# Cross-attention and a mixture of experts on one core: experts chosen in groups of four tiles, and another order of work in the late attention

## The chip, the cores and the metric

One core of a Trainium2 chip runs the whole kernel in one launch. The metric is the time of an execution on the device in microseconds (us). The kernel before was run three times: 351.25, 352.0 and 418.66 us, median 352.0. The profiled execution is the one of 351.25 us; its span from the first to the last instruction is 349.4 us.

Engines as in the profile: PE is TensorE (matmuls), PEld its weight loads, DVE is VectorE, ACT is ScalarE, POOL is GpSimd, SP is the engine that issues most DMAs.

## The reference

x is 32 tiles of 128 tokens with 256 channels, in float32. Per token the reference computes a layer normalisation, and an attention over the token's own 16 heads of 16 channels: Q from the normalised token, K and V from the context token at the same place, a 16 by 16 matrix of logits, softmax, values, the output projection Wd, and the residual. Then, on a second layer normalisation, it chooses one of 8 experts per token (argmax of 8 gate logits), runs that expert's two-layer network (256 to 512 to 256, exact GELU), scales by the softmax score and adds the residual.

```python
query = q @ Wq.T + bq; key_p = k @ Wk.T + bk; value = v @ Wv.T + bv     # heads: (.., 16, 16)
logits = einsum('bsid,bsjd->bsij', query, key_p) / sqrt(16)
out = einsum('bsij,bsjd->bsid', softmax(logits), value) @ Wd.T + bd
x = x + out
idx, scores = argmax(gates), max(gates)            # gates = softmax(layernorm(x) @ w_red @ wg_n.T)
o = gelu(h @ W1[idx] + b1[idx]) @ W2[idx] + b2[idx]
x = x + o * scores
```

## The kernel before

Attention runs in iterations t = 0 to 41 (`*_attention` on each engine), software-pipelined: every engine has its own written order of work, and semaphores tie them together. Iteration t treats several tiles at once. Tile t is projected to K, V and Q (`tensor_project`, L1088, L1091, L1185), evicted by VectorE (`vector_kv` L599, `vector_q` L605, L610), stored to a scratch in HBM by SP and loaded back in another layout. Tile z = t-5 has its K expanded by GpSimd with a mask (`pool_expand`, L413) and its V copied by ScalarE (`scalar_pad`, L973). Tile s0 = t-6 gets its logits (L1100), the row maximum (L631) and subtraction (L633) on VectorE, the exponential on ScalarE (L927), and the sum, reciprocal and product on VectorE (`normed`, L566, L569, L573). Tile s1 = t-7 is transposed (`tensor_turn`, L1197), expanded with a mask in four blocks (`expand` on VectorE, L558, `scalar_expand` on ScalarE, L996, one instruction a block), multiplied with V (L1111) and copied out by ScalarE (L950). Tile w = t-8 gets the output projection (L1143), the residual (L644), the largest gate logit (L649) and, on GpSimd, the gate logits less the largest (L452). Tile d = t-9 gets its norm from a power on GpSimd (L430, L432, L435) that waits for ScalarE's moments (L902) of the iteration before, and ScalarE's score row (`scalar_row`). Its row goes to HBM by SP (`sync_row`). GpSimd also adds the bias to tile t-2's residual (L449) and reorders a context tile (`pool_context`, L398).

Who expands which block is told by `blocks`: in the steady iterations ScalarE has 3 and VectorE 1, from iteration 27 (ROUTE) ScalarE has all 4, in 34 and 35 (FIRST = 34) each has 2, then VectorE all. VectorE comes first, ScalarE waits for it. Outside iterations 32 and 33 ScalarE's blocks follow its exponential.

Experts are worked on in slots of 128 rows. The first 13 slots (S1) are filled from the first 20 tiles (R1), so that their routing can run during the attention: `vector_early` with parts 0 to 7. Part 0 (iteration 28) chooses the expert of all 20 tiles (L692, L693, L694); TensorE counts (`tensor_counts_a`); part 1 (end of 28) turns the counts into prefixes and full tiles (L698 to L705); parts 2, 3, 4 (iterations 29, 30, 31) work out every token's place (L707 to L722) and the list of experts (L723 to L726); parts 5 and 6 (32, 33) build selection matrices (L730 to L736), TensorE inverts the list with 20 small matmuls (`tensor_inverse_a`, L1223) and part 7 (34) turns the result into addresses (L744, L745). GpSimd's first gather (`pool_ffn(0)`, L497) of iteration 34 needs these. `after` makes each step wait for the one before. `PIECES` makes GpSimd's K expansion of iterations 28 to 34 wait for VectorE's part of that iteration.

`FILLS` are filler transposes of the identity (L1059) that nobody reads, {7: 16, 32: 6, 33: 6, 35: 6} before the values matmul. From iteration 36 the expert slots run: rows transposed (L1290), first layer (L1278), GELU (L1051), second layer (L1328), bias and score (L889, L895), scatter (L472); weights are copied by L859 or L1032.

## Time and profile before

| what | value |
|---|---|
| median of the runs | 352.0 us |
| time of the profiled execution | 351.25 us |
| its span | 349.4 us |
| PE busy | 326.0 us, 93% of the span |
| DVE busy | 250.7 us, 72% |
| ACT busy | 200.4 us, 57% |
| POOL busy | 270.2 us, 77% |
| chain that ended last | PE 69%, DVE 9%, DMA 8%, issue 5%, ACT 4%, POOL 3% |
| moved by DMA | 63.46 MB, mean 182 GB/s |

The shares are means over stages that have different limits. The chain that ended last is followed back from the last instruction: at each step to what released it, or to the instruction before it on its engine. "issue" is time in which the engine waited for nothing that the profile shows. The timeline gives each instruction, or a few alike, with its start and duration; the stretch table gives busy time, granted TensorE clock (1.00 is full speed, 2.4 GHz) and the DMA engines' busy share between two times.

### The profile page before, as it was taken

Reading aid. Unit: us, or ns where it says so; the run is one execution under the profiler, and the core shown is the slowest. Engines: PE = TensorE matmul, PEld = TensorE weight load, DVE = VectorE, ACT = ScalarE, POOL = GpSimd, SP = SyncE. Lnnn points to the kernel's source line nnn. Section 1 sums busy time; section 2 is a strip of 40 time slices with the busy share of each in tenths; the row PEclk is TensorE's granted clock in tenths of the full one; section 3 lists DMA queues with packets and bytes.
Section 4 is the critical chain, followed back from the end, with each engine's and each line's share of the span. In section 5 each row is a group of like instructions: output and inputs, shape, how many; then the busy total and the mean of one; then the engine's idle time right before and its main releaser. Section 6 shows DMA issues by size and latency. Waiting matters only on the chain.

```text
span 349.4 us, 11007 instructions
## 1 busy us (share of the span) xinstructions
PE 326.0 (93%) x3731; PEld 273.2 (78%) x3731; DVE 250.7 (72%) x717; ACT 200.4 (57%) x533; POOL 270.2 (77%) x523
## 2 busy tenths in 40 slices
PE   6999899999999999899687899979999999999993
PEld 5787788888888888677476688968898999995682
DVE  6656788888888888899777656875765566554652
ACT  1001678777877787578754745784567535435431
POOL 3598789999999899787888767774778777777634
PEclk9999999999999999999969999999999999999998
DMA  6699898999999999999997111251122222222200
GB/s 223 233 294 301 264 217 249 268 301 271 264 270 262 291 328 322 340 237 251 303 364 289 50 33 46 68 153 48 46 76 66 77 65 73 77 61 74 62 15 31
DMA packets 54839, 63.46 MB, mean 182 GB/s; under 512 B 36334, under 2 KB 45695, under 8 KB 54784
## 3 DMA queue, kind: packets, MB, share of 16 engines
q1 hardware_dynamic: 50544, 52.77, 51.8%
q0 software_dynamic: 3456, 9.12, 8.8%
q10 hardware_dynamic: 784, 0.87, 0.7%
q8 instruction: 31, 0.51, 0.6%
q14 instruction: 24, 0.20, 0.2%
HBM read 41.59 MB, written 21.68 MB: 181 GB/s over the span
## 4 chain that ended last, share of the span: by engine, by line
PE 69%; DVE 9%; DMA 8%; issue 5%; ACT 4%; POOL 3%; ACTq 1%; SPq 1%; DVEq 0%; POOLq 0%
PE bQ L1328 14%; PE bY L1143 7%; PE bKV L1091 7%; PE bKV L1088 7%; PE bQ L1185 7%; PE bKV L1278 6%; PE bL L1278 6%; PE bO L1111 4%; PE bL L1100 4%; PE bA L1197 3%; DMA r<-row_scr,ig 3%; PE bT L1290 2%; DMA xt<-in_x 2%; DMA r<-in_xc 2%; DMA b2b<-in_bd_col 1%
## 5 line engine op out<-in xcount | busy, mean ns | idle before, releaser
L1328 PE MATMUL bQ<-w,wA 128*128 x264 | 63.2, 382 | 2.1 <-issue 1.2
L413 POOL TENSOR_TENSOR x<-ql,mask 128x1024 f32<-128x1024 f32 x32 | 60.6, 1893 | 4.7 <-DVE texp L726 1.7
L1328 PEld LDWEIGHTS bQ<-w,wA 128*128 128x128 f32 x264 | 47.5, 190 | 9.5 <-issue 4.3
L472 POOL DMA_INDIRECT out<-r,isc x36 | 38.7, 1074 | 19.6 <-issue 17.6
L973 ACT ACTIVATE pad<-ql 64x512 f32<-64x512 f32 x64 | 40.0, 626 | 22.3 <-DMA ql<-qkv_scr 21.9
L889 DVE TENSOR_TENSOR r<-bQ,b2b 128x256 f32<-128x256 f32 (+1 forms) x39 | 16.6, 425 | 36.2 <-PE bQ L1328 34.3
L497 POOL DMA_INDIRECT r<-row_scr,ig x36 | 37.4, 1038 | 5.7 <-issue 2.4
L996 ACT ACTIVATE ax<-bA,mask 128x256 f32<-128x256 f32 x92 | 36.7, 474 | 0.7 <-DVE ax L558 0.5
L1143 PE MATMUL bY<-wD,oT 128*128 128x265 f32 x128 | 35.7, 402 | 1.0 <-ACT oT L950 0.8
L1278 PEld LDWEIGHTS bL<-wA,r 128*128 128x128 f32 x272 | 32.7, 192 | 2.4 <-issue 1.7
L1278 PE MATMUL bL<-wA,r 128*128 128x128 f32 x272 | 33.4, 276 | 1.1 <-ACT r L1032 1.1
L1185 PE MATMUL bQ<-wA,r 128*128 128x265 f32 x128 | 33.9, 387 | 0.3 <-DVE wA L533 0.3
L1088 PE MATMUL bKV<-wA,r 128*128 128x256 f32 x128 | 33.0, 380 | 1.1 <-DMA r<-in_xc 0.7
L1091 PE MATMUL bKV<-wA,cp 128*128 128x256 f32 x128 | 33.1, 381 | 0.0
L927 ACT ACTIVATE bX<-bL 128x256 f32<-128x256 f32 x32 | 11.8, 370 | 36.9 <-DVE bL L633 36.9
L432 POOL TENSOR_TENSOR cat<-ve,half 128x2 f32<-128x2 f32 x42 | 30.2, 720 | 3.5
L1051 ACT ACTIVATE wA<-bL,r 128x128 f32<-128x128 f32 x68 | 19.4, 373 | 22.1 <-PE bL L1278 22.1
L1278 PEld LDWEIGHTS bKV<-wA,r 128*128 128x128 f32 x256 | 30.8, 192 | 1.2 <-issue 0.4
L1278 PE MATMUL bKV<-wA,r 128*128 128x128 f32 x256 | 31.5, 276 | 0.0
L1051 ACT ACTIVATE wA<-bKV,r 128x128 f32<-128x128 f32 x64 | 18.2, 366 | 21.1 <-PE bKV L1278 21.0
L1007 ACT ACTIVATE r<-r 128x256 f32<-128x256 f32 x36 | 22.0, 611 | 11.2 <-DMA r<-row_scr,ig 10.9
L1185 PEld LDWEIGHTS bQ<-wA,r 128*128 128x128 f32 x128 | 24.1, 189 | 4.3 <-DVE wA L533 0.4
(214 smaller groups left out, 703.6 us busy)
## 6 DMA issues: line engine op xcount, KB each, us to landing
qkv_scr<-qkv SPq DMA_DIRECT2D x16, 768.0 KB, 4.4
ql<-qkv_scr SPq DMA_DIRECT2D x32, 384.0 KB, 5.8
r<-in_xc SPq DMA_DIRECT2D x15, 512.0 KB, 6.0
row_scr<-cat SPq DMA_DIRECT2D x32, 133.5 KB
w1b<-in_W1b SPq DMA_DIRECT2D x8, 514.0 KB, 7.3
w<-in_W SPq DMA_DIRECT2D x8, 512.0 KB
xt<-in_x SPq DMA_DIRECT2D x15, 256.0 KB, 6.0
b2b<-in_b SPq DMA_DIRECT2D x2, 512.0 KB, 8.2
```

The source lines that it names most:

```text
L413: eng.tensor_tensor(quarter(kx[:, z % 2, :]), spread(ql[z // 2 % 2][:, :, z % 2, 0:HD]), mask_k, ALU.mult).then_inc(S["kx"], 1)
L472: eng.indirect_dma_start(out, bass.IndirectOffsetOnAxis(ap=isc[k][:, :], axis=0), yo[k], None, bounds_check=NTOK - 1, oob_is_err=False).th ...
L497: eng.indirect_dma_start(gr[k], None, row_scr[0:R1 * P] if a < S1 else row_scr, bass.IndirectOffsetOnAxis(ap=ig[k][:, :], axis=0)).then_in ...
L973: i_ = eng.activation(pad[n, z % 3, :].rearrange("p (k g h d) -> p k g h d", k=2, g=NG_, h=2) [:, :, :, h, :], ql[z // 2 % 2][n, :, z % 2, ...
L996: i_ = eng.activation(quarter(ax[:, :])[:, :, b, :], bA[:, 0:C].rearrange("p (g i) -> p g i", g=NG_), ACT.Copy, scale=mask4[:, b:b + 1])
L1051: i_ = eng.activation(hT[a % 2][:, k, :], bH[a % 2][:, k * P:(k + 1) * P], ACT.Gelu, bias=w1s[a % 2][:, KC * HID + k:KC * HID + k + 1])
L1088: eng.matmul(bKV[:, 0:C], xcT[:, a % XC, KC + k, :], wT[:, k, 0:C], start=(k == 0), stop=(k == KC - 1))
L1091: i_ = eng.matmul(bKV[:, C:2 * C], cp[a % 2][:, k, :], wT[:, k, C:2 * C], start=(k == 0), stop=(k == KC - 1))
L1143: i_ = eng.matmul(bY[:, 0:EXT], oT[:, k, :], wD[:, k, :], start=(k == 0), stop=(k == KC - 1))
L1185: i_ = eng.matmul(bQ[:, 0:EXT], xcT[:, a % XC, k, :], wT[:, k, 2 * C:3 * C + NL], start=(k == 0), stop=(k == KC - 1))
L1278: i_ = eng.matmul(bH[a % 2][:, k * P:(k + 1) * P], w1s[a % 2][:, c * HID + k * P:c * HID + (k + 1) * P], gT[a % 2][:, c, :], start=(c == 0 ...
L1328: i_ = eng.matmul(bQ[:, 0:C], hT[b % 2][:, k, :], w2[:, bass.ds(eb * (KH * C) + k * C, C)], start=(k == 0), stop=(k == KH - 1))
```

## The change

The choice of experts is cut into five groups of four tiles: `vector_choice(g)` runs in iterations 13, 17, 21, 25 and 28 (`GROUP_AT`), after the residual of that iteration. Part 1 of the early routing copies the prefixes out of PSUM before it scans, and rounds the counts to whole tiles by adding and subtracting a large constant, in place of a comparison and a sum. TensorE's output projection of iteration 29 waits for the scan. The list of experts (end of part 4) and the number taken (end of part 6) become part 8, in iteration 34 after the softmax; part 7, the addresses, moves ahead of the residual of iteration 34.

In `scalar_attention`, the blocks of iteration 7 and of 32 to 35 come ahead of the exponential, V's copies of iterations 32 on come behind it, and the output copy of 32 to 35 comes ahead of the moments. In 34 and 35 VectorE's blocks wait for ScalarE's. Iteration 7's four blocks are all ScalarE's. GpSimd's K expansion of iterations 32 and 33 comes behind the power; its waits on pieces of the routing end with iteration 31. The filler transposes become {7: 10, 32: 4, 33: 4, 35: 4}.

```diff
...
 STEADY = FIRST + 2
-FILLS = {7: 16, 32: 6, 33: 6, 35: 6}
+FILLS = {7: 10, 32: 4, 33: 4, 35: 4}
 FILLS_ROWS = 8
...
 BLOCKS_STEADY, BLOCKS_ROUTING, BLOCKS_DRAIN = 3, 4, 2
+TURNED_FIRST = (7, *range(NT, STEADY))
+OUTPUT_FIRST = range(NT, STEADY)
 SELR = NH2 + 2
-PIECES = (("gsub", R1), ("rv_a", 5), ("rv_a", 10), ("rv_a", 13), ("texp_a", 1), ("selk_a", 1), ("taken_a", 1))
+GROUP = 4
+GROUPS = R1 // GROUP
+GROUP_AT = {min(GROUP * g + 13, ROUTE + 1): g for g in range(GROUPS)}
+SCANNED = 2 * GROUPS + 1
+RV_COUNTS = SCANNED + 2
+PIECES = (("gsub", R1), ("rv_a", RV_COUNTS), ("rv_a", RV_COUNTS + 5), ("rv_a", RV_COUNTS + 8))
 
...
                 n, v, w, d, z = t + 1, t - 2, t - 8, t - 9, t - 5
-                if live(z) and t >= NT:
+                if t >= FIRST and live(z):
                     pool_expand(eng, t, z)
...
                     pool_constants(eng)
-                if live(z) and t < NT:
+                if live(z) and t < FIRST:
                     pool_expand(eng, t, z)
...
                 return 0
-            return BLOCKS_DRAIN if s1 + 7 >= FIRST else BLOCKS_ROUTING if s1 + 7 >= ROUTE else BLOCKS_STEADY
+            return BLOCKS_DRAIN if s1 + 7 >= FIRST else BLOCKS_ROUTING if s1 + 7 >= ROUTE or s1 == 0 else BLOCKS_STEADY
 
...
                 eng.wait_ge(S["tr_a"], s1 + 1)
+                if 0 < b and s1 + 7 in TURNED_FIRST:
+                    eng.wait_ge(S["axs"], by_scalar(s1))
                 if s1 > 0:
...
                     expand(eng, s1)
+                if t == ROUTE + 7:
+                    vector_early(eng, 7)
                 if live(s0) and t <= ROUTE:
...
                     normed(eng, s0)
-                if t == ROUTE + 1:
-                    vector_early(eng, 0)
+                if t in GROUP_AT:
+                    vector_choice(eng, GROUP_AT[t])
                 if live(a) and t >= 7:
...
                         vector_stats(eng, a + 2)
-                if ROUTE + 1 < t <= ROUTE + 7:
+                if ROUTE + 1 < t < ROUTE + 7:
                     vector_early(eng, t - ROUTE)
+                if t == ROUTE + 7:
+                    vector_early(eng, 8)
                 if live(a) and t >= 7:
...
 
-        def vector_early(eng, part):
+        def routed(eng):
             def after(i_):
...
                 eng.wait_ge(S["rv_a"], rv_a[0])
-
-            if part == 0:
+            return after
+
+        def vector_choice(eng, g):
+            after = routed(eng)
+            n = slice(GROUP * g, GROUP * (g + 1))
+            if g == 0:
                 eng.wait_ge(S["const"], 1)
                 eng.wait_ge(S["wide"], 2)
-                eng.wait_ge(S["gsub"], R1)
-                after(eng.scalar_tensor_tensor(key_a, glog[:, 0:R1, :], 0.0, io_e[:, 0:R1, :], ALU.is_ge, ALU.mult))
-                after(eng.tensor_reduce(top_a, key_a, AX, ALU.max))
-                eng.tensor_tensor(oh[:, 0:R1, :], key_a, top_a.unsqueeze(2).broadcast_to((P, R1, NE)),
-                                  ALU.is_equal).then_inc(S["oh_a"], 1)
+            eng.wait_ge(S["gsub"], GROUP * (g + 1))
+            after(eng.scalar_tensor_tensor(key_a[:, n, :], glog[:, n, :], 0.0, io_e[:, n, :], ALU.is_ge, ALU.mult))
+            after(eng.tensor_reduce(top_a[:, n], key_a[:, n, :], AX, ALU.max))
+            eng.tensor_tensor(oh[:, n, :], key_a[:, n, :], top_a[:, n].unsqueeze(2).broadcast_to((P, GROUP, NE)),
+                              ALU.is_equal).then_inc(S["oh_a"], 1)
+
+        def vector_early(eng, part):
+            after = routed(eng)
             if part == 1:
                 eng.wait_ge(S["cnt_a"], 1)
+                eng.tensor_copy(pre_a, bA[:, C:C + NE * R1].rearrange("p (e n) -> p e n", e=NE)
+                                ).then_inc(S["cnt_r"], 1)
                 after(eng.tensor_tensor_scan(inc_a.rearrange("p e n -> p (e n)"),
...
                                              bY[:, EXT:EXT + NE * R1], 0.0, ALU.mult, ALU.add))
-                eng.tensor_copy(pre_a, bA[:, C:C + NE * R1].rearrange("p (e n) -> p e n", e=NE)
-                                ).then_inc(S["cnt_r"], 1)
-                after(eng.scalar_tensor_tensor(gtm_a, inc_a[:, :, R1 - 1:R1].broadcast_to((P, NE, R1)), 1.0 - P,
-                                               io_m[:, :, 0:R1], ALU.add, ALU.is_gt))
-                after(eng.tensor_reduce(full, gtm_a, AX, ALU.add))
+                after(eng.tensor_scalar(fexc, inc_a[:, :, R1 - 1], (1.0 - P) / 2, ROUND, ALU.add, ALU.add))
+                after(eng.tensor_scalar(full, fexc, ROUND, None, ALU.subtract))
             if part == 2:
...
                 after(eng.tensor_tensor(fexc, finc, full, ALU.subtract))
-                after(eng.tensor_scalar(pinc, finc, float(P), float(S1 * P), ALU.mult, ALU.min))
-                after(eng.scalar_tensor_tensor(exc_a, fexc.unsqueeze(2).broadcast_to((P, NE, R1)), float(P), inc_a,
-                                               ALU.mult, ALU.add))
+                after(eng.tensor_scalar(pinc, finc, float(S1 * P), None, ALU.min))
+                after(eng.tensor_tensor(exc_a, fexc.unsqueeze(2).broadcast_to((P, NE, R1)), inc_a, ALU.add))
                 eng.wait_ge(S["cnt_r"], 1)
...
                 after(eng.tensor_tensor(posr_a, pos_a, posk_a, ALU.subtract))
+            if part == 8:
                 after(eng.tensor_tensor(tcmp_a, pinc.unsqueeze(1).broadcast_to((P, S1, NE)),
...
                 eng.tensor_scalar(texp[:, 0:S1], tsum_a, float(NE - 1), None, ALU.min).then_inc(S["texp_a"], 1)
+                after(eng.tensor_scalar(pexc, fexc, float(S1 * P), None, ALU.min))
+                eng.tensor_tensor(taken[:, :], pinc, pexc, ALU.subtract).then_inc(S["taken_a"], 1)
             if part in (5, 6):
...
                                   ALU.mult).then_inc(S["selk_a"], 1)
-            if part == 6:
-                after(eng.tensor_scalar(pexc, fexc, float(P), float(S1 * P), ALU.mult, ALU.min))
-                eng.tensor_tensor(taken[:, :], pinc, pexc, ALU.subtract).then_inc(S["taken_a"], 1)
             if part == 7:
...
                 a, z, s0, s1, w, d = t, t - 5, t - 6, t - 7, t - 8, t - 9
-                if live(z) and t >= NT:
-                    scalar_pad(eng, z)
-                if live(s1) and shared(s1) and NT <= t < FIRST:
+                if live(s1) and t in TURNED_FIRST:
                     scalar_expand(eng, s1)
...
                                    ACT.Exp, scale=HD ** -0.5).then_inc(S["exp"], 1)
-                if live(s1) and shared(s1) and not NT <= t < FIRST:
+                if live(s1) and shared(s1) and t not in TURNED_FIRST:
                     scalar_expand(eng, s1)
-                if live(z) and t < NT:
+                if live(z):
                     scalar_pad(eng, z)
...
                         scalar_weights(eng, s)
+                if live(s1) and t in OUTPUT_FIRST:
+                    scalar_output(eng, s1)
                 if live(w):
...
                     scalar_row(eng, t, d)
-                if live(s1):
-                    eng.wait_ge(S["pvo"], s1 + 1)
-                    if s1 > 0:
-                        eng.wait_ge(S["wd"], s1)
-                    eng.activation(oT[:, :, :].rearrange("p m (i b) -> p m i b", i=NH),
-                                   bO[:, 0:C].rearrange("p (m b i) -> p m i b", m=KC, i=NH),
-                                   ACT.Copy).then_inc(S["oT"], 1)
+                if live(s1) and t not in OUTPUT_FIRST:
+                    scalar_output(eng, s1)
                 for s in SLOTS_AT.get(t, ()):
...
                 eng.wait_ge(S["score"], d + 1)
+
+        def scalar_output(eng, s1):
+            eng.wait_ge(S["pvo"], s1 + 1)
+            if s1 > 0:
+                eng.wait_ge(S["wd"], s1)
+            eng.activation(oT[:, :, :].rearrange("p m (i b) -> p m i b", i=NH),
+                           bO[:, 0:C].rearrange("p (m b i) -> p m i b", m=KC, i=NH),
+                           ACT.Copy).then_inc(S["oT"], 1)
 
...
             eng.wait_ge(S["tr_a"], s1 + 1)
-            if blocks(s1) < NC_:
+            if blocks(s1) < NC_ and s1 + 7 not in TURNED_FIRST:
                 eng.wait_ge(S["axv"], by_vector(s1))
...
                     eng.wait_ge(S["oT"], w + 1)
+                    if t == ROUTE + 2:
+                        eng.wait_ge(S["rv_a"], SCANNED)
                     for k in range(KC):
...
         def tensor_counts_a(eng):
-            eng.wait_ge(S["oh_a"], 1)
+            eng.wait_ge(S["oh_a"], GROUPS)
             eng.wait_ge(S["const"], 1)
...
             eng.matmul(bY[:, EXT:EXT + NE * R1], ones[:, :], ohe_a, start=True, stop=True).then_inc(S["cnt_a"], 1)
```

## Rows read from the trace of the kernel before

**Rows 1.** Stretches: length, busy PE PEld DVE ACT POOL, clock, DMA share, GB/s

```profile
100.00:141.00 41.00, 41.00 (x724) 33.92 (x724) 36.16 (x108) 32.32 (x85) 37.13 (x68) 1.00 1.04 296
...
170.00:190.00 20.00, 16.08 (x295) 13.11 (x294) 14.72 (x41) 11.60 (x31) 17.96 (x27) 0.83 1.05 355
...
177.30:182.60 5.30, 5.26 (x76) 4.53 (x76) 3.17 (x10) 3.41 (x9) 4.72 (x7) 0.50 1.00 361
```

**Rows 2.** The chain of waits, whole span: start us, us, what

```profile
57.11 0.91 PE bY L1143 x4
...
140.98 1.04 PE bY L1143 x4
...
148.18 0.90 PE bY L1143 x4
...
153.44 1.13 PE bY L1143 x4
...
164.54 1.89 POOL x L413
...
169.75 1.57 ACT ax L996 x4
...
179.15 1.25 POOL r L497
...
185.42 5.83 DMA r<-row_scr,ig
```

**Rows 3.** The timeline of a steady iteration: start us, us, engine, line, operation

```profile
51.87 0.42 DVE L631 TENSOR_REDUCE mx<-bL 128x16 f32<-128x256 f32 x1
...
52.83 1.89 POOL L413 TENSOR_TENSOR x<-ql,mask 128x1024 f32<-128x1024 f32 x1
...
54.90 0.69 DVE L599 TENSOR_TENSOR qkv<-bKV,bqkv 128x512 f32<-128x512 f32 x1
...
55.15 0.75 POOL L449 TENSOR_TENSOR xt<-xt,bdb 128x265 f32<-128x265 f32 x1
...
56.11 0.63 PE L1100 MATMUL bL<-x,pad 128*32 128x64 f32 x32
...
56.81 0.42 DVE L631 TENSOR_REDUCE mx<-bL 128x16 f32<-128x256 f32 x1
```

**Rows 4.** The timeline of iterations 28 and 29

```profile
143.74 0.45 DVE L692 SCALAR_TENSOR_TENSOR r<-glog,io_e 128x160 f32<-128x160 f32 x1
...
144.31 0.74 POOL L449 TENSOR_TENSOR xt<-xt,bdb 128x265 f32<-128x265 f32 x1
...
144.59 0.65 DVE L694 TENSOR_TENSOR oh<-r 128x160 bf16<-128x160 f32 x1
...
148.31 0.42 DVE L631 TENSOR_REDUCE mx<-bL 128x16 f32<-128x256 f32 x1
```

**Rows 5.** Groups of VectorE instructions by line: count, busy us, mean ns

```profile
L761 DVE TENSOR_TENSOR oh<-pad 128x96 bf16<-128x96 f32 x1 | 0.2, 250 | 0.0
...
L709 DVE TENSOR_SCALAR r<-r 128x8 f32<-128x8 f32 x1 | 0.2, 172 | 0.0
...
L703 DVE SCALAR_TENSOR_TENSOR r<-r,io_m 128x160 f32<-128x160 f32 x1 | 0.3, 317 | 0.0
```

**Rows 6.** The timeline of iterations 31 to 34

```profile
163.59 0.27 DVE L723 TENSOR_TENSOR r<-r,io_k 128x104 f32<-128x104 f32 x1
...
166.70 0.72 POOL L432 TENSOR_TENSOR cat<-ve,half 128x2 f32<-128x2 f32 x1
...
171.42 0.65 PE L1111 MATMUL bO<-ax,pad 128*32 128x64 f32 x32 [0.92 <-issue]
...
175.09 1.35 PE L1223 MATMUL bKV<-r 128*128 128x26 bf16 x20
...
178.11 0.17 DVE L745 SCALAR_TENSOR_TENSOR idg<-bKV,r 128x13 int32<-128x13 f32 x1
```

**Rows 7.** The timeline of iteration 8's beginning, TensorE

```profile
41.30 0.65 PE L1100 MATMUL bL<-x,pad 128*32 128x64 f32 x32 [0.45 <-issue]
```

## The prediction

> **What bounds the kernel now.** I read the stretch table first [rows 1]. Between 100 and 141 us TensorE is busy for all 41.00 us at full clock: the steady attention iterations are bound by its matmuls. The other engines are not idle either: VectorE is busy 36.16 of 41.00, GpSimd 37.13, and the DMA engines are full. Then the chain of waits [rows 2]: the output projection L1143 starts at 57.11 in iteration 11 and at 140.98 in iteration 28, so 17 iterations take 83.87 us, 4.93 each. The next two take 7.20 (to 148.18) and 5.26 (to 153.44). From 141 to about 192 the chain leaves TensorE: it goes over GpSimd's K expansion at 164.54, ScalarE's four blocks at 169.75, GpSimd's first gather at 179.15 and the landing of the second, issued at 185.42 and 5.83 us under way. After that it is TensorE's expert matmuls again. So this change, which touches iterations 7, 13 to 28 and 28 to 35, can win between 141 and 192 us and can lose in the steady part.
>
> How much room the steady part has is read from one iteration [rows 3]. The row maximum L631 starts at 51.87, and the projection of the next iteration must start at 57.11 [rows 2]: 5.24 us. What that path needs is seen in iteration 29, where VectorE sets the pace: L631 at 148.31 [rows 4], the projection at 153.44 [rows 2], 5.13 us with four blocks on ScalarE. Four blocks take 1.57 [rows 2], 0.39 each; with three the path is 4.74, and some 0.1 more for the wait on VectorE's own block. So L631 may come about 0.4 late before TensorE waits. VectorE itself is idle 4.84 us in 8.3 iterations [rows 1], 0.58 each, mostly the short gaps between dependent instructions; I estimate 0.2 as true spare ahead of L631 at 56.81 [rows 3].
>
> **Part by part. Choices in groups, steady part.** In iterations 13, 17, 21 and 25 VectorE gets three dependent instructions of 32 elements between L649 and L599 at 54.90. Of 96 elements one costs 0.25, of 8 elements 0.17 [rows 5]: 0.19 each, 0.6 together, if nothing is in the way. Something is: GpSimd's residual bias L449 runs from 55.15 to 55.90 [rows 3], where the third would run. In iteration 28 the same instruction, L694, ran beside L449 and took 0.65 [rows 4]; 96 elements without company took 0.25 [rows 5], so 160 should take 0.32. It ended at 145.24, 0.19 after L449. Put at 55.35, it would end near 56.09 in place of 55.55: 1.1 us are inserted. So L631 is late by 0.4 (0.6 less the spare 0.2) up to 0.9, and TensorE loses 0 to 0.5 per group. I take 0.3, nearer the hindered end since that is the row I have: four groups, **+1.2** (0 to +2.0). Who else stands behind it on VectorE: K/V eviction L599, the statistics for GpSimd's power, the Q eviction and with it SP's store of the record (all four iterations are odd). Each of these has its reader an iteration or more away, so I cost them at nothing; GpSimd's K expansion, which would come 1 us late, ends 1.4 ahead of its logits today (52.83 + 1.89 against 56.11 [rows 3]). The groups are four iterations apart, enough to lose the lag again.
>
> The Trainium skill ("SBUF — State Buffer", section "SBUF: two separate sides") says that VectorE and GpSimd share one pair of ports by an exclusive lock, which a VectorE instruction with two SBUF inputs needs and for which the loser fully blocks. L694 and L449 agree with it. By that rule alone each group would cost its full 0.5, and the sum below would be 0.8 higher.
>
> **Iteration 28.** Before, L692 at 143.74 to the end of L694 at 145.24 is 1.50 [rows 4]; a group of four takes 0.6 to 1.3 there, again beside L449. I take 0.3 saved (0.15 to 0.9). The count of full tiles replaces L703 (0.32) and a reduction as long by two instructions of 8 elements at 0.17 [rows 5]: 0.3. The copy out of PSUM goes ahead of the scan, so the transposes no longer wait for the scan; the projection now waits for it instead, and behind that wait stand TensorE's K/V and Q matmuls. The scan is over as early as before, so this costs nothing by itself; if it came late it would cost its own half microsecond. L631 of iteration 29 comes 0.6 early.
>
> **Iteration 31.** Three instructions of the expert list, from L723 at 163.59 [rows 6], 0.7 together, leave the space ahead of the Q eviction. They return in iteration 34, after the softmax. With the 0.6 the next L631 is 1.3 early. Parts 2 and 3 keep their number of instructions.
>
> **Iterations 32 and 33.** Today GpSimd waits for that list before K (164.54 [rows 2]), the power L432 follows at 166.70 [rows 6], the moments wait for it and the output copy for the moments; ScalarE fills V ahead of its blocks, which start at 169.75 [rows 2], and the values matmul of iteration 33 is at 171.42 [rows 6]. With the new order the blocks start when the transposes are done, near 168.0, and the values matmul near 169.65: 1.8 early. K comes later in GpSimd's order, by power and its product, 1.3 us. It starts near 164.6, as now, and TensorE gets logits only 0.5 early. V's copies, two of 0.63 per tile, lie after the exponential and end about when K does. SP's load of the last record waits for its store's landing, not for these. The output copy goes ahead of the moments, which feed the next power; with the power early they still end before GpSimd gets there. In 34 and 35 VectorE's two blocks wait for ScalarE's two instead of the other way round: the same two pieces in the other order, 0.
>
> The waits of K on the pieces fall away from iteration 32 on, so K may now hold up the selection matrices. Nothing in the trace has them side by side; from below it costs nothing, from above the rest of a K expansion, 1.9. Two GpSimd instructions (K's tail and L449) can meet it: I take 0.5.
>
> **Iteration 34.** The inverse matmul goes from 175.09 [rows 6] to about 173.7. The addresses L745, at 178.11 now, stand behind the residual, its maximum and the softmax, 1.7 us; ahead of them they come 1.4 after the matmuls start and are done near 175.5, 2.7 early. For that VectorE stands 0.8 idle with the residual queued behind, which still starts earlier than now. GpSimd can use 2.7 only if it is free: K, power and product end near 176.0 to 176.8. The first gather is issued near 177.2 instead of 179.15 [rows 2], the second 1.9 before its 185.42 [rows 2], and what follows hangs on the second one's landing. **−1.9** for 141 to 192 us, all of the parts above together (−1.2 to −2.7).
>
> **Iteration 7 and the filler transposes.** The first tile's four blocks go ahead of the exponential. I estimate the values 0.5 early, but the softmax 0.9 late, and VectorE's lateness reaches V's copies two tiles on. The wait of 0.45 before the logits at 41.30 [rows 7] shrinks. 0 (−0.3 to +0.2). The 12 filler transposes that go run while TensorE would wait anyway: 0, as long as the clock stays up (below). Without it they would be a loss.
>
> **Sum.** The profiled execution took 351.25 us for its span of 349.4. 351.25 + 1.2 − 1.9 = **350.6**. The median of the runs before is 352.0, 0.75 above the profiled one.
>
> **Rivals.** A, the slower side: the lock beside L449. Every group costs 0.5 (+2.0), and the selection matrices meet K so that only 1.2 comes back: 352.1. It decides when the third instruction of a group starts after 55.15 within its iteration. For: L694's 0.65. Against: the spare of VectorE is only estimated. 0.22.
> B, all groups fit: 3 x 0.19 stays under the room, GpSimd is free at 176: 351.25 − 2.7 = 348.6. For: TensorE never waits for VectorE in the steady part. Against: L449. 0.25.
> C, the gathers land when the DMA engines have worked off the weights: between 170 and 190 us these are fully busy at 355 GB/s [rows 1], and a gather takes 5.83 there. If the second lands at 191.2 whatever its issue, both gain and steady loss vanish: 351.2. Against: the weights too are issued earlier. 0.12. The Trainium skill ("DMA: Bandwidth & Descriptors", section "Queues, rings and completion order") has each DMA engine go round between its queues packet by packet, which speaks for a constant delay and against C; the landing after a shifted issue will tell.
> D, fewer fillers: the granted clock was 0.50 from 177.3 to 182.6 [rows 1], 1.2 GHz, after a stretch where TensorE waited and ran small matmuls. Cut shorter still, it could fall already at the inverse; its 1.35 us and the values behind it at half rate give back 1.5: 352.1. 0.08.
> My forecast: 0.33, with its own range 349.8 to 351.4.
>
> **The numbers.** Below 348.2 the whole gain would need more than B; above 353.0 more than A's. 8 in 10 lie between. What a measurement of this kernel can tell from no change is about 2%, 7 us, and all cases lie within it: 0.96; 0.02 on either side for what I have not seen.
>
> **What would show it.** Right: projection starts 4.93 apart except 0.3 more after iterations 13, 17, 21, 25; in 28 to 29 6.6 instead of 7.20; the first gather's issue 1.9 before the rest of the shift, the second landing 5.8 after its issue. Wrong: equal distances throughout (B); third instruction over 0.5 and steps of 0.5 (A); a second landing that has not moved (C); half clock before the addresses (D); or K or the bias on GpSimd delayed by the unguarded selections by more than 1 us.

## The result, and the profile after

The changed kernel takes 355.15 us (median of 6 runs, 354.54 to 358.72), the kernel before 351.85 in the same comparison: 1.0119 times as long, 95% interval 1.0082 to 1.0156. It is slower by 1.2%. The forecast was 350.6 with a range up to 353.0: a gain was forecast, a loss came, and it lies beyond the range. The profiled execution took 354.97 us against 351.25 before, 3.7 more.

The page of the changed kernel, busy time by engine and the chain that ended last:

```profile
PE 328.1 (93%) x3719; PEld 273.1 (77%) x3719; DVE 257.4 (73%) x728; ACT 200.8 (57%) x534; POOL 271.2 (77%) x523
...
PE 69%; DVE 7%; POOL 7%; issue 6%; DMA 6%; ACT 4%; DVEq 0%; SPq 0%; ACTq 0%; POOLq 0%
```

VectorE is busy 6.7 us longer than before (257.4 against 250.7), though the eleven more instructions that it has (728 in place of 717) are worth some 0.2 us each. Instructions became longer, not only more. The stretch table (columns as in [rows 1]) says where TensorE waits. Below, "K" is short for GpSimd's K expansion, and two instructions "meet" or "collide" where one of VectorE and one of GpSimd run at the same time and one of them takes much longer than it does elsewhere.

```profile
100.00:141.00 41.00, 40.57 (x659) 32.93 (x658) 36.42 (x110) 30.93 (x81) 36.39 (x65) 1.00 0.98 278
...
170.00:192.00 22.00, 15.81 (x273) 12.46 (x266) 20.16 (x41) 12.29 (x33) 18.44 (x27) 0.84 1.02 339
```

From 100 to 141 us TensorE was busy for all 41.00 us [rows 1], now 40.57: it has begun to wait. From 170 to 192 it is busy for 15.81 of 22.00, and VectorE for 20.16.

**The ledger.** I compared the start of the projection's weight load (PEld L1143 before, L1166 now) in each iteration. The table gives its shift against the kernel before in us (plus is later), worked out from the timelines; the later columns are the experiments below, each from one profiled run of its own.

```
iteration    after   e3 one   e5 spread  e4 behind  e2 no 7  e1 guards  e7 both  c1
 8           -0.04   -0.43    -0.23      -0.19      -0.07    -0.05      -0.14    +1.52
 9           +0.48   +0.10    +0.30      +0.34      -0.07    +0.48      -0.14    +1.52
27           +3.09   +0.09    +0.29      +1.05      +2.44    +2.96      -0.15    +1.59
30           +1.84   -0.11    -0.25      +0.45      +1.83    +3.04      -0.46    +0.43
34           +0.60   -1.47    -1.49      -0.80      +0.46    +1.56      -1.84    -0.92
36           +3.81   +1.84    +1.88      +2.57      +3.59    +1.47      -1.94    -0.99
38           +4.43   +1.90    +2.34      +3.08      +4.29    +1.83      -1.58    -0.69
```

In the changed kernel iteration 7 costs 0.5, the four groups 2.6 (0.52, 0.66, 0.65 + 0.14, 0.64), iterations 28 and 29 give back 1.2, the way to iteration 34 another 1.2, and then two iterations lose 3.2 and two more 0.6. The expert slots give back 0.7, which leaves 3.7.

**The first group**, iteration 13 of the changed kernel, from the timeline (columns as in [rows 3]):

```profile
70.22 0.31 DVE L709 SCALAR_TENSOR_TENSOR r<-glog,io_e 128x32 f32<-128x32 f32 x1
70.45 0.66 POOL L456 TENSOR_TENSOR xt<-xt,bdb 128x265 f32<-128x265 f32 x1
70.56 0.19 DVE L710 TENSOR_REDUCE r<-r 128x4 f32<-128x32 f32 x1
70.78 0.37 DVE L711 TENSOR_TENSOR oh<-r 128x32 bf16<-128x32 f32 x1
...
71.07 0.68 DVE L608 TENSOR_TENSOR qkv<-bKV,bqkv 128x512 f32<-128x512 f32 x1
...
72.14 0.75 PEld L1166 LDWEIGHTS bY<-wD,oT 128*128 128x128 f32 x4
...
72.76 0.41 DVE L640 TENSOR_REDUCE mx<-bL 128x16 f32<-128x256 f32 x1
...
77.59 0.52 PEld L1166 LDWEIGHTS bY<-wD,oT 128*128 128x128 f32 x3 [0.32 <-issue]
```

The third instruction, L711, meets the bias add L456 and ends with it. The eviction L608 starts 1.43 after the residual at 69.64; in iterations without a group it is 0.54. The next row maximum comes at 72.76, 0.67 later than 4.93 after the one at 67.16, and the two projections are 5.45 apart instead of 4.93. In iteration 21, as in 17 and 25, the same collision is at its full size, with the eviction 1.55 after the residual and the next row maximum 0.79 late:

```profile
111.13 0.74 POOL L456 TENSOR_TENSOR xt<-xt,bdb 128x265 f32<-128x265 f32 x1
111.26 0.66 DVE L711 TENSOR_TENSOR oh<-r 128x32 bf16<-128x32 f32 x1
```

**Iterations 33 to 36** of the changed kernel, VectorE and GpSimd with TensorE's inverse and one projection:

```profile
170.58 0.22 DVE L757 TENSOR_TENSOR r<-r,io_n 128x130 bf16<-128x130 bf16 x1
...
175.34 1.89 POOL L420 TENSOR_TENSOR x<-ql,mask 128x1024 f32<-128x1024 f32 x1
175.36 1.95 DVE L757 TENSOR_TENSOR r<-r,io_n 128x130 bf16<-128x130 bf16 x1
...
177.37 0.77 PE L1246 MATMUL bKV<-r 128*128 128x26 bf16 x10 [0.94 <-DVE r L757]
...
178.81 0.17 DVE L763 SCALAR_TENSOR_TENSOR idg<-bKV,r 128x13 int32<-128x13 f32 x1
...
179.71 1.25 POOL L504 DMA_INDIRECT r<-row_scr,ig  x1 [0.19 <-issue]
180.62 2.71 DVE L742 TENSOR_TENSOR r<-r,io_k 128x104 f32<-128x104 f32 x1
181.01 0.31 POOL L459 TENSOR_SCALAR glog<-cat,gm 128x8 f32<-128x8 f32 x1
181.30 1.89 POOL L420 TENSOR_TENSOR x<-ql,mask 128x1024 f32<-128x1024 f32 x1
...
187.02 1.12 POOL L504 DMA_INDIRECT r<-row_scr,ig  x1 [0.17 <-issue]
187.89 2.75 DVE L877 TENSOR_SCALAR r<-w1b 128x1028 f32 x1 [0.71 <-issue]
188.17 1.90 POOL L420 TENSOR_TENSOR x<-ql,mask 128x1024 f32<-128x1024 f32 x1
190.05 0.67 POOL L437 TENSOR_SCALAR ve<-va 128x2 f32<-128x2 f32 x1
```

Three VectorE instructions are held up while K (L420) runs: the first two end 0.08 and 0.14 after it, the third 0.57 after it. The last product for the selection matrices, L757, takes 1.95 where the same line took 0.22 an iteration earlier; ten of the twenty inverse matmuls wait for it. The list's comparison L742 takes 2.71 where it took 0.27 before (L723 in [rows 6]). The copy of the first expert's weights, L877, takes 2.75; before the line took 0.70. That is 1.7 + 2.4 + 2.05 us of VectorE, and the chain of waits goes through them (start us, us, what); the third shows as "issue" while VectorE holds the weight copy:

```profile
175.45 1.86 DVE r L757
...
180.70 2.63 DVE r L742
...
187.95 2.61 issue
```

### The profile page after: what moved, and what is told of

Same layout as the page of the kernel before. It is cut to its first block, busy times and chain, and to the rows that moved or that the text cites. A ratio compares the mean times of both kernels' runs of the same rounds, so it can differ in the third digit from the quotient of the medians.

```text
span 353.1 us, 10994 instructions
## 1 busy us (share of the span) xinstructions
PE 328.1 (93%) x3719; PEld 273.1 (77%) x3719; DVE 257.4 (73%) x728; ACT 200.8 (57%) x534; POOL 271.2 (77%) x523
## 4 chain that ended last, share of the span: by engine, by line
PE 69%; DVE 7%; POOL 7%; issue 6%; DMA 6%; ACT 4%; DVEq 0%; SPq 0%; ACTq 0%; POOLq 0%
PE bQ L1351 12%; PE bKV L1112 7%; PE bQ L1208 7%; PE bKV L1109 7%; PE bY L1166 7%; PE bL L1301 6%; PE bKV L1301 5%; PE bO L1132 4%; PE bL L1121 4%; PE bA L1220 3%; PE bT L1313 2%; DMA wA<-in_wkvT 2%; DMA r<-in_xc 2%; DMA r<-row_scr,ig 2%; PE bQ L1344 2%
## 5 line engine op out<-in xcount | busy, mean ns | idle before, releaser
L420 POOL TENSOR_TENSOR x<-ql,mask 128x1024 f32<-128x1024 f32 x32 | 60.6, 1894 | 2.2 <-issue 0.2
L504 POOL DMA_INDIRECT r<-row_scr,ig x36 | 38.3, 1063 | 5.6 <-issue 2.1
L1166 PE MATMUL bY<-wD,oT 128*128 128x265 f32 x128 | 35.7, 402 | 0.6
L877 DVE TENSOR_SCALAR r<-w1b 128x1028 f32 x27 | 20.9, 775 | 12.3 <-issue 8.8
L1112 PEld LDWEIGHTS bKV<-wA,cp 128*128 128x128 f32 x128 | 24.0, 189 | 4.6 <-POOL cp L405 1.3
```

Source lines behind the costliest of these rows:

```text
L420: eng.tensor_tensor(quarter(kx[:, z % 2, :]), spread(ql[z // 2 % 2][:, :, z % 2, 0:HD]), mask_k, ALU.mult).then_inc(S["kx"], 1)
L504: eng.indirect_dma_start(gr[k], None, row_scr[0:R1 * P] if a < S1 else row_scr, bass.IndirectOffsetOnAxis(ap=ig[k][:, :], axis=0)).then_in ...
L1112: i_ = eng.matmul(bKV[:, C:2 * C], cp[a % 2][:, k, :], wT[:, k, C:2 * C], start=(k == 0), stop=(k == KC - 1))
L1166: i_ = eng.matmul(bY[:, 0:EXT], oT[:, k, :], wD[:, k, :], start=(k == 0), stop=(k == KC - 1))
```

## The experiments

Ratios are to the kernel before, on the same chip, with 95% intervals. The medians of the kernel before were 351.59 us beside e1, e2, e3 and e5, 351.13 beside e4, e6, e7 and c1, 351.89 beside f1 and f2.

**e1: K waits for VectorE's pieces again.** This asks what it costs that K meets the selection matrices and the list.

```
-PIECES = (("gsub", R1), ("rv_a", RV_COUNTS), ("rv_a", RV_COUNTS + 5), ("rv_a", RV_COUNTS + 8))
+PIECES = (("gsub", R1), ("rv_a", RV_COUNTS), ("rv_a", RV_COUNTS + 5), ("rv_a", RV_COUNTS + 8),
+          ("rv_a", RV_COUNTS + 12), ("selk_a", 1), ("selk_a", 2), ("taken_a", 1))
```

> The changed kernel, but GpSimd's K expansion of iterations 32 to 35 waits for VectorE's routing piece of that time again (places done, first selection, second selection, number taken). Theory (a), that most of what is lost after iteration 33 is VectorE's two-input instructions being held up by K (L757 1.95 us where 0.22 is its time alone, L742 2.71 where 0.27 is): the pieces take their own time again, iterations 34 and 35 shrink by 2 to 4 us, 352.0 us. Theory (b), that these instructions are only where a wait shows that comes from somewhere else (addresses, gathers, clock): K starts later by as much as it waits, and the time stays at 355 us or rises.

Measured: 353.23 us, ratio 1.0036 [1.0009, 1.0063]. That is a miss of 1.2 against the 352.0 of theory (a), but this interval and the changed kernel's (1.0082 to 1.0156) do not overlap. GpSimd and VectorE of e1 in the same place:

```profile
176.73 1.89 POOL L421 TENSOR_TENSOR x<-ql,mask 128x1024 f32<-128x1024 f32 x1 [0.39 <-DVE r L758]
...
180.05 0.26 DVE L743 TENSOR_TENSOR r<-r,io_k 128x104 f32<-128x104 f32 x1
...
182.42 1.89 POOL L421 TENSOR_TENSOR x<-ql,mask 128x1024 f32<-128x1024 f32 x1
...
184.88 0.70 DVE L878 TENSOR_SCALAR r<-w1b 128x1028 f32 x1 [0.71 <-issue]
```

K waits 0.39 us for L758, and in exchange all three collisions are gone. The ledger reads the price: from iteration 30 to 38 e1 goes from +3.04 to +1.83, the changed kernel from +1.84 to +4.43. By these two runs the missing waits cost 3.8 us there. The two profiled times differ by only 1.2 (354.97 against 353.75), since e1's profiled run also lost the gain of iterations 28 and 29: in 28 its VectorE waited 1.28 us for a row's store, which no other profiled run's did. The two ratios differ by 0.0083, 2.9 us.

**f1: the same waits without the last one.** The last wait lies in iteration 35, behind the inverse. Is it needed, or does the first collision bring on the others? The edit against e1:

```
-          ("rv_a", RV_COUNTS + 12), ("selk_a", 1), ("selk_a", 2), ("taken_a", 1))
+          ("rv_a", RV_COUNTS + 12), ("selk_a", 1), ("selk_a", 2))
```

> The changed kernel with K's waits back in iterations 32, 33 and 34, but none in 35, where the late list of experts (L742) and then the weight copy (L877) met K. Theory (a), each collision is its own loss: L757 takes 0.22 us again and 1.7 us come back there, L742 still takes over 2 us; between the kernel with all waits (353.2) and the changed one (355.2): 354.2 us. Theory (b), the selection's collision alone sets the addresses and so all that follows: 353.2 us, the wait in 35 is worth nothing.

Measured: 352.68 us, 1.0025 [0.9991, 1.006], not distinguishable from e1, nor from the kernel before. The list and the weights of f1 stay clear of K without a wait:

```profile
179.45 0.26 DVE L743 TENSOR_TENSOR r<-r,io_k 128x104 f32<-128x104 f32 x1
...
184.75 0.70 DVE L878 TENSOR_SCALAR r<-w1b 128x1028 f32 x1 [0.90 <-issue]
```

K of iteration 35 starts at 181.82 and the next at 187.72. So the waits of iterations 32 to 34 suffice. That the first collision pushes VectorE into the later two fits both runs; a kernel with the wait of 34 alone was not run.

**e6: the kernel before, without K's last three waits.** The same suspicion with nothing else of the change.

```
-PIECES = (("gsub", R1), ("rv_a", 5), ("rv_a", 10), ("rv_a", 13), ("texp_a", 1), ("selk_a", 1), ("taken_a", 1))
+PIECES = (("gsub", R1), ("rv_a", 5), ("rv_a", 10), ("rv_a", 13))
```

> The kernel before, with one thing of the change: GpSimd's K expansion of iterations 32, 33 and 34 no longer waits for VectorE's routing pieces. Theory (a), VectorE's two-input instructions lose their port to K: list, selections and number taken meet K in at least two iterations, 1.7 us each; iterations 32 to 34 become 2 to 3 us longer, 353.5 us. Theory (b), K starts earlier by the waits of 1.7, 0.5 and 0.3 us that fall away, and that is the gain meant: 350.5 us.

Measured: 353.33 us, 1.0051 [1.0017, 1.0085]: 1.8 us slower. The timeline of e6 shows three collisions:

```profile
162.81 1.90 POOL L413 TENSOR_TENSOR x<-ql,mask 128x1024 f32<-128x1024 f32 x1
162.96 1.78 DVE L720 TENSOR_SCALAR r<-r 128x20 f32<-128x20 f32 x1
...
168.17 1.89 POOL L413 TENSOR_TENSOR x<-ql,mask 128x1024 f32<-128x1024 f32 x1
...
168.84 1.90 DVE L730 TENSOR_TENSOR r<-io_r,r 128x1280 bf16<-128x1280 bf16 x1
...
173.02 1.90 POOL L413 TENSOR_TENSOR x<-ql,mask 128x1024 f32<-128x1024 f32 x1
...
173.70 1.90 DVE L730 TENSOR_TENSOR r<-io_r,r 128x1280 bf16<-128x1280 bf16 x1
```

L720 is 20 elements wide and has one input; it took 1.78 us in place of 0.18. L730 took 1.90 twice, in place of 0.93 and 0.82. K's three waits in the kernel before (1.70, 0.49 and 0.27 us, the first for L726, at 164.54) look like a loss in the profile and together are worth more than they cost.

**e3: one choice of 20 tiles in iteration 28**, all else as changed. This asks what the groups cost.

```
-GROUP = 4
+GROUP = R1
...
-GROUP_AT = {min(GROUP * g + 13, ROUTE + 1): g for g in range(GROUPS)}
+GROUP_AT = {ROUTE + 1: 0}
```

> The changed kernel with the choice of all 20 tiles in one piece at iteration 28, everything else of the change kept. Theory (a), that the four groups of the steady part cost 0.5 to 0.65 us each because TensorE has no room for 0.9 us more on VectorE: steps of 4.93 us throughout to iteration 28, 2.6 us won there, and 0.8 lost again in iteration 28 by the longer piece; 353.3 us. Theory (b), that the groups lose only as much as iteration 28 gains: 355 us. Theory (c), that DMA is the limit behind both: 355 us with the loss moved to later iterations.

Measured: 353.16 us, 1.0041 [1.0016, 1.0066]. The steady part has no step left: its shift is +0.10 in iteration 9 and +0.09 in 27. The price is that iterations 28 and 29 give back only 0.2, since the wide third instruction meets the bias add there as it did before:

```profile
144.51 0.74 POOL L456 TENSOR_TENSOR xt<-xt,bdb 128x265 f32<-128x265 f32 x1
144.54 0.89 DVE L711 TENSOR_TENSOR oh<-r 128x160 bf16<-128x160 f32 x1
```

**e4: the groups behind the statistics.** The same three instructions in one piece in the same iterations, but after `vector_stats`, where GpSimd's bias add is over. This tells the work of a group from its collision.

```
...
-                if t in GROUP_AT:
+                if t == ROUTE + 1:
                     vector_choice(eng, GROUP_AT[t])
                 if live(a) and t >= 7:
                     vector_kv(eng, a)
                     if live(a + 2):
                         vector_stats(eng, a + 2)
+                if t in GROUP_AT and t <= ROUTE:
+                    vector_choice(eng, GROUP_AT[t])
```

> The changed kernel with each group's three instructions in one piece, but behind the statistics instead of behind the residual. Theory (a), the collision with GpSimd's bias add makes the loss: inserted are 0.6 us instead of 0.9 to 1.1, and the loss per group falls from 0.52 to 0.65 to 0.1 at most: iteration 28 starts 0.3 to 0.5 late against before instead of 3.0; 352.9 us. Theory (b), the length of one piece makes it (0.6 against room of 0.36 + 0.2): 0.05 to 0.1 per group. Theory (c), any wait chain of three makes it: 0.5 per group, 355 us. The power on GpSimd (0.72 us, two inputs) starts just then and could take the bias add's place: then 0.5 again.

Measured: 353.83 us, 1.0061 [1.0031, 1.0092]. The four steps are 0.24, 0.15, 0.16 and 0.16 us, more than the 0.1 at most that theory (a) gave them and far less than the 0.52 to 0.66 of the changed kernel. The timeline of e4, iteration 13:

```profile
70.31 0.66 POOL L456 TENSOR_TENSOR xt<-xt,bdb 128x265 f32<-128x265 f32 x1
...
71.30 0.19 DVE L711 SCALAR_TENSOR_TENSOR r<-glog,io_e 128x32 f32<-128x32 f32 x1
...
71.53 0.19 DVE L712 TENSOR_REDUCE r<-r 128x4 f32<-128x32 f32 x1
...
71.75 0.19 DVE L713 TENSOR_TENSOR oh<-r 128x32 bf16<-128x32 f32 x1
```

So of 0.65 us a group, some 0.16 is its work and some 0.5 the collision.

**e5: one instruction of a group per iteration**, behind the statistics. `vector_choice` gets a third argument that says which of its three instructions it issues.

```
...
+                for g in range(GROUPS - 1):
+                    if 0 <= t - (GROUP * g + 12) < 3:
+                        vector_choice(eng, g, t - (GROUP * g + 12))
...
```

> The changed kernel, with the three instructions of a group one per iteration (4g+12, 4g+13, 4g+14) and behind the statistics, where GpSimd's bias add is over. If the loss per group is made by a piece longer than the spare time of one iteration (0.36 + 0.2 us), 0.2 us each fit and the steady part keeps 4.93 us: 352.5 us, with iteration 28's gain kept. If it is made by the collision with GpSimd's bias add alone, the same. If any added work on VectorE costs TensorE its length, 0.2 x 12 = 2.4 us stay: 355 us.

Measured: 352.96 us, 1.0034 [1.001, 1.0059]. The shift stays at +0.3 from iteration 9 to 27: a single instruction of 0.19 us behind the statistics fits into the steady iteration, three in one piece (e4) do not quite.

**e2: iteration 7 as before**, with its 16 fillers.

```
-FILLS = {7: 10, 32: 4, 33: 4, 35: 4}
+FILLS = {7: 16, 32: 4, 33: 4, 35: 4}
...
-TURNED_FIRST = (7, *range(NT, STEADY))
+TURNED_FIRST = (*range(NT, STEADY),)
...
-            return ... BLOCKS_ROUTING if s1 + 7 >= ROUTE or s1 == 0 else BLOCKS_STEADY
+            return ... BLOCKS_ROUTING if s1 + 7 >= ROUTE else BLOCKS_STEADY
```

> The changed kernel with iteration 7 as before: ScalarE three blocks behind the exponential, VectorE one, 16 filler transposes. Theory (a), that VectorE's softmax came 1 us late there and V's copy held up logits and projection of iteration 9: the projection of iteration 9 comes 0.48 us earlier and the end with it, 354.6 us. Theory (b), that this loss is taken up later anyway by the DMA engines' backlog: the projections move, the end does not, 355.1 us.

Measured: 356.11 us, 1.0113 [1.0067, 1.016], not distinguishable from the changed kernel. The 0.55 us are won by iteration 9 (-0.07 against +0.48) and gone by iteration 30 (+1.83 against +1.84). The third instruction of the last group and the bias add, first in e2 and then in the changed kernel:

```profile
146.58 0.75 POOL L456 TENSOR_TENSOR xt<-xt,bdb 128x265 f32<-128x265 f32 x1
146.69 0.69 DVE L711 TENSOR_TENSOR oh<-r 128x32 bf16<-128x32 f32 x1
```

```profile
147.19 0.19 DVE L711 TENSOR_TENSOR oh<-r 128x32 bf16<-128x32 f32 x1
147.29 0.75 POOL L456 TENSOR_TENSOR xt<-xt,bdb 128x265 f32<-128x265 f32 x1
```

In both kernels the next eviction, L608, starts at 147.30. Who comes first, by 0.1 us, decided 0.5 us (0.69 against 0.19 for L711). The changed kernel's gain in iteration 28 is partly this luck.

**f2: the changed kernel with the old number of fillers** (16, 6, 6, 6), for rival D.

```
-FILLS = {7: 10, 32: 4, 33: 4, 35: 4}
+FILLS = {7: 16, 32: 6, 33: 6, 35: 6}
```

> The changed kernel with the filler transposes as before (16, 6, 6, 6). If fewer fillers let the clock fall earlier or longer (it stood at half for parts of 177 to 191 us in the changed kernel), the half clock is shorter and the time 354 us. If the clock falls by TensorE's waiting for VectorE in 34 and 35, where the fillers are few either way, it stays as it was and the time at 355 us; 6 more transposes in iteration 7 and 2 in each of the others lie in waits and cost nothing.

Measured: 356.04 us, 1.0132 [1.006, 1.0203], no better than the changed kernel. Its mean granted clock was 0.987, the changed kernel's 0.988, and e1's, with the fewer fillers too, 0.999. Fewer fillers did not cost the clock.

**e7 and c1: the collisions avoided.** e7 is the changed kernel with e1's waits, one choice (e3) and iteration 7 as before (e2). c1 takes e5's spread groups instead of the one choice.

> The changed kernel with one choice of 20 tiles at iteration 28, iteration 7 as before and all of K's waits: what is left of the change is the order of the late attention, the shorter part 1 and the late list of experts. If that order is worth what was forecast, steps as before to iteration 28, then 0.3 us won there and 1 to 2 us up to the second gather: 350 us. If the order of the late attention by itself loses (K behind the power in 32 and 33, VectorE standing for the inverse matmul): 352 to 353 us.

> Three repairs together: K's waits back, one instruction of a group per iteration behind the statistics, iteration 7 as before. If the three losses are separate they add up: steady part as before, 1.1 us won by iteration 29, no instruction of VectorE held up by K: 349.5 us, faster than the kernel before. If the lost time comes back elsewhere (landing of the gathers, clock): 351 to 352 us.

Measured: e7 350.25 us, 0.9951 [0.992, 0.9983]; c1 350.11 us, 0.9952 [0.9924, 0.998]. Both are faster than the kernel before, by 0.5%. What is left of the change in e7 is the new part 1, the late order and the fewer fillers of iterations 32 to 35. Its ledger goes from -0.15 in iteration 27 to -0.46 in 30 and -1.58 in 38. The timeline of e7:

```profile
174.84 0.17 DVE L764 SCALAR_TENSOR_TENSOR idg<-bKV,r 128x13 int32<-128x13 f32 x1
...
176.65 0.26 DVE L743 TENSOR_TENSOR r<-r,io_k 128x104 f32<-128x104 f32 x1
...
177.42 1.25 POOL L505 DMA_INDIRECT r<-row_scr,ig  x1 [0.19 <-issue]
...
182.87 0.70 DVE L878 TENSOR_SCALAR r<-w1b 128x1028 f32 x1 [0.75 <-issue]
...
183.78 1.12 POOL L505 DMA_INDIRECT r<-row_scr,ig  x1 [0.17 <-issue]
```

The addresses are there at 174.84 instead of 178.11 [rows 6], the gathers go out at 177.42 and 183.78 instead of 179.15 and 185.42 [rows 2]: 1.7 and 1.6 earlier. And the second gather's landing moved with its issue, in the chain of waits of e7:

```profile
183.78 5.80 DMA r<-row_scr,ig
```

c1's ledger starts at +1.5 because its profiled run's first loads landed later. From iteration 27 to 38 it gives back 2.3, e7 1.4; 0.85 of that difference arises by iteration 30, where c1's last small group ran ahead of the bias add. In the medians the two are equal.

## Why the prediction was wrong, step by step

**The choices in groups, +1.2 forecast, +2.6 measured.** The mechanism was named, as rival A with a chance of 0.22. The step that failed is the price of one group, 0.3 where 0.65 came, and two numbers of it were wrong. First, of "0 to 0.5" I took 0.3, although the only row that showed the third instruction in that place, L694 beside L449 [rows 4], was the hindered one; the same row put 1.1 us in front of the eviction, and 0.9 came in the first group, 1.0 in the other three. Second, the room of TensorE was read as 0.4 and is 0.2. I subtracted a start in the timeline (51.87) from one in the chain of waits (57.11, [rows 2]). The timeline of the kernel before puts the same matmuls at 56.95:

```profile
56.95 1.08 PE L1143 MATMUL bY<-wD,oT 128*128 128x265 f32 x4
```

That is 5.08 us from the row maximum, not 5.24. The path itself was right: from the maximum at 72.76 to the projection's matmuls at 77.63 it took 4.87, 4.84 forecast. The spare of VectorE was right too: 0.89 inserted, 0.67 of it late at the maximum, so 0.22 was spare where 0.2 was estimated. With the room of 5.08 - 4.87 = 0.21 the first group gives 0.67 - 0.21 = 0.46, the others, 0.79 to 0.82 late at the maximum, 0.58 to 0.61. In e4 the maximum is 0.39 late in the first group and 0.31 in the others, which gives 0.18 and 0.10. Measured were 0.52 and 0.64 to 0.66, and in e4 0.24 and 0.15 to 0.16: every step is some 0.05 more than this sum. That the groups are "four iterations apart, enough to lose the lag again" held: the lag of 0.67 to 0.82 is gone before the next group.

The Trainium skill ("SBUF — State Buffer", section "SBUF: two separate sides"), cited beside this step, gave the sum that is nearer. It has whoever starts first keep the ports for the whole instruction, and e2 against the changed kernel agrees: with the bias add first by 0.11 us L711 took 0.69, with L711 first by 0.10 us it took 0.19.

**All from 141 us on, -1.9 forecast, +0.6 measured** (from +3.09 in iteration 27 to the 3.7 of the profiled times). The step that failed is the price of "The waits of K on the pieces fall away from iteration 32 on", for which the prediction says "I take 0.5". By iteration 38 the ledger against e1 puts the price at 3.8 us. To the end of the execution it is 2.4: the profiled times differ by 1.2, and e1 had lost the 1.2 of iterations 28 and 29. The same sum of e3 against e7 gives 2.8. f1, which leaves out only a wait that did not hold K, gives 1.7 by its profiled run and 3.3 by its ratio (1.0025 against 1.0119), and e6 1.8 on the kernel before. So the price is some 2 to 3 us, at least four times what was taken and mostly over the upper bound of 1.9. The bound counted one K expansion, as if K could be met once. It was met three times, and each time it held a VectorE instruction until it was over. Two of these three were not on my list: the list's own instructions, which the change moves into iteration 34 in front of a K expansion, and the weight copy of the first slot. And the bound was for what stands behind one K expansion, while L742 was held over the end of the gather's issue, the gate subtraction and all of K. e6 shows that a price of this kind belongs to the waits and not to the new order.

The working of -1.9 follows the gathers and shows no place for the 0.5, although the text counts it in. -1.9 with the measured 2.4 on top is +0.5, and +0.6 came.

**The new order itself was priced about right.** With the waits kept, e7 goes from -0.15 in iteration 27 to -2.13 in its profiled time (349.12 against 351.25): -2.0, where -1.9 was forecast. That so near a hit is partly luck: this run was the fastest of e7's ten. The medians differ by 0.9 (350.25 against 351.13), and the ratio makes it 1.7 with an interval of 0.6 to 2.8. The gain is shown, its size only roughly; the forecast had -1.2 to -2.7. In the trace of e7 the addresses came 3.3 earlier (forecast 2.7), the first gather 1.7 and the second 1.6 (forecast 1.9). The moved list and the addresses ahead of the residual did what was said.

**Iteration 28 and part 1, -0.6 forecast.** The changed kernel got 1.2, of which some 0.6 came from the last group slipping in ahead of the bias add. Without this luck (e2, e4, e5, f1) it is 0.5 to 0.6, as forecast; with it (c1, f2) 1.2; with one choice (e3, e7) 0.2 to 0.3.

**Iteration 7, 0 forecast with -0.3 to +0.2.** It cost 0.5 in the ledger. The values came 0.3 early (39.87 against 40.20), but the softmax ended 1.2 late (40.78 against 39.61 for its product, forecast 0.9). The next row maximum was still 0.8 late (42.81 against 42.01), the logits of iteration 9 0.3 and its projection 0.5. The wait before the logits at 41.26 grew to 0.74, where it was to shrink. e2 wins the 0.5 and is no faster, because it loses the lucky order of iteration 28 in exchange; the 0 holds for the wrong reason.

**The rivals.** A's mechanism was the right one, and even its sum, 352.1, was 3 us short: it still had the late part win 1.2, which lost 0.6, and it took 0.5 for a group, which cost 0.65. B needed groups that fit; e5 shows that it takes one instruction per iteration. C fell: in e7 the second gather had landed at 189.58, 1.7 ahead of the 191.2 that C would have kept, 5.80 after its issue against 5.83 before [rows 2]. D fell with f2, and the half clock came later, not earlier: the granted clock of the changed kernel is 0.50 from 181 to 183 us and 0.54 from 189 to 191, where it was 0.50 from 177.3 to 182.6 before [rows 1]. Both follow a stretch in which TensorE often waited, mostly for VectorE: it was busy for 1.02 us of 177 to 179, and for 0.65 of 185 to 187.

**What stays open.** Why a row's store landed late in e1's profiled run; it was seen once. How much of the price of the missing waits is TensorE's half clock that follows the idle stretches: e1's profiled run had none, f1's some (mean 0.993), and their medians do not differ. Which of the three meetings costs how much at the end: they were only taken away together. Whether the ports of the Trainium skill are what holds the instructions: the runs show that the meetings cost time and how much, not the port.

## What to carry to other kernels

Before taking away a wait, list every instruction of the two engines that it kept apart, in all the iterations that follow, and price each meeting at the whole longer instruction: on the kernel before, three waits of 2.46 us together were cheaper than the three meetings that they prevent. Put small VectorE work where GpSimd is idle in the steady schedule, not where the code reads best; here this is worth 0.5 us each time. And take both ends of a room from the same view: start times of one matmul differed by 0.16 us between the chain of waits and the timeline, which was half of the room.

## What the runs showed of the hardware that was not expected

- A VectorE instruction can be kept out by several GpSimd instructions in a row. L742 (104 elements, two inputs) began at 180.62 under the gather's issue, which ended at 180.96. L459 started at 181.01 and K at 181.30, and L742 ended at 183.33, 0.14 after K. It is not always so: L751 of the changed kernel began at 169.42 beside the bias add, which ended at 169.52, and was through at 170.23, and here the next GpSimd instruction, L459 at 169.49, took 0.98 in place of some 0.3. The Trainium skill ("SBUF — State Buffer", section "SBUF: two separate sides") speaks of one instruction that blocks the other; L742 was kept out by three.
- Instructions with one input were held as well: L877 (128x1028 in float32) took 2.75 instead of 0.70, L720 of e6 (20 elements) 1.78 instead of 0.18. The Trainium skill ("VectorE: DVE Perf Modes", section "What auto-detection actually checks") has a mode 2×_2P for a single source and a destination in SBUF. If that mode takes both ports, it would explain the two; no run here tells the modes apart.
- Not every VectorE instruction is held. The reciprocal L578 (one input, 128x16 in float32) and the product L582, whose larger input lies in PSUM, ran at 172.88 and 173.24 in the changed kernel, beside the K of 171.99 to 173.88, and took 0.25 and 0.42, as in the other iterations (0.25 or 0.26, and 0.42).
- The reverse happens too: L437 on GpSimd, 0.22 elsewhere, took 0.67 beside the end of L877, and the power L440 of e1 1.03 instead of 0.72.
